# Both attention phases of neighbouring batches in common slots, in a decoder layer on one core

## What is computed

```python
x = _layernorm(x + _L0_attn_ref(x, ...))          # relu(x Wqkv); vk = v^T k; y = (vk q) / den; y Wp + b
x = _layernorm(x + _L0_xattn_ref(x, ctx_1024, ctx_1024, pos, pos, ...))
    # q = x Wq, k = ctx Wk, v = ctx Wv; q, k to float16 and rotated; softmax(q k^T / 4) v; Wo + b
x = _layernorm(x + _L0_ffn_ref(x, ...))           # x U1 V1 + b1, gelu, U2 V2 + b2
```

## Time and profile before

| | us |
|---|---|
| median of 3 runs | 634.99 (631.4 to 635.81) |
| profiled execution | 636.95 |
| its span, from the first to the last instruction | 635.0 |
| PE busy in the span | 555.6 |
| DVE busy | 464.2 |
| ACT busy | 312.4 |
| POOL busy | 286.8 |

### The profile page before, as it was taken

The page is one execution under the profiler, slowest core; times in us unless marked ns, Lnnn a source line. Parts: engine busy times, 40 slices in busy tenths (PEclk is TensorE's granted clock), DMA queues, the critical chain, the costliest instruction groups (busy, mean ns, idle before and its releaser), DMA issues.

```text
span 635.0 us, 12707 instructions
## 1 busy us (share of the span) xinstructions
PE 555.6 (87%) x4288; PEld 369.3 (58%) x4288; DVE 464.2 (73%) x974; ACT 312.4 (49%) x455; POOL 286.8 (45%) x300
## 2 busy tenths in 40 slices
PE   0867799899999999999999999999996958999993
PEld 0755557575757575766657575757573524455561
DVE  4377569898988888889889798989887672244434
ACT  4321173645545463646373736455454626656561
POOL 3471535454546454637364554545453401224334
PEclk9886599999999999999999999999999877999998
DMA  7526200201020202020201111010000000033322
GB/s 251 124 69 131 64 6 10 67 9 67 8 66 8 66 8 67 7 70 11 66 18 58 39 35 63 11 66 8 34 9 18 26 1 17 18 106 121 104 99 100
DMA packets 24029, 33.77 MB, mean 53 GB/s; under 512 B 4552, under 2 KB 10440, under 8 KB 24008
## 3 DMA queue, kind: packets, MB, share of 16 engines
q1 hardware_dynamic: 23192, 33.07, 17.2%
q10 hardware_dynamic: 816, 0.43, 0.3%
HBM read 22.73 MB, written 8.65 MB: 49 GB/s over the span
## 4 chain that ended last, share of the span: by engine, by line
PE 61%; issue 10%; DVE 9%; ACT 8%; POOL 4%; POOLq 0%; DVEq 0%; ACTq 0%
PE FR L1013 14%; PE BK L1013 12%; PE BK L1174 9%; PE SC L1157 5%; DVE nmax L857 5%; PE SC L1133 5%; ACT probs L634 3%; PE FR L1081 3%; PE FR L1089 3%; PE FR L1071 3%; PE FR L1215 3%; PE BK L1185 2%; POOL rs L536 2%; POOL c_fm L541 2%; ACT x_fm L623 2%
## 5 line engine op out<-in xcount | busy, mean ns | idle before, releaser
L857 DVE TENSOR_REDUCE nmax<-SC 128x4 f32<-128x1024 f32 x128 | 149.8, 1216 | 12.4 <-PE SC L1133 12.3
L634 ACT ACTIVATE probs<-SC 128x1024 f32<-128x1024 f32 x128 | 124.3, 1033 | 19.5 <-PE SC L1157 19.5
L1174 PE MATMUL BK<-probs,v_aug 128*32 128x256 f32 x1024 | 69.5, 389 | 0.0
L1133 PE MATMUL SC<-k_blk,q_grp 32*128 32x512 f16 x256 | 49.2, 402 | 12.6 <-DVE nmax L857 12.6
L442 POOL TENSOR_TENSOR att_fm_l<-att_raw,att_fm_h 128x512 fp32r<-128x512 f32 x16 | 20.6, 1286 | 74.1 <-ACT att_raw L615 74.1
L1157 PE MATMUL SC<-q_grp,k_blk 64*128 64x256 f16 x512 | 45.9, 279 | 9.0 <-ACT probs L634 8.4
L696 ACT ACTIVATE probs<-SC,b_ff 128x512 f32<-128x512 f32 x64 | 39.6, 688 | 24.4 <-PE SC L1338 23.7
L431 POOL TENSOR_TENSOR k_cos<-k,cos_t 128x512 f16<-128x512 f16 x16 | 18.5, 1154 | 69.4 <-ACT k L591 69.4
L1174 PEld LDWEIGHTS BK<-probs,v_aug 128*32 128x32 f32 x1024 | 26.9, 110 | 28.2 <-issue 10.9
L838 DVE TENSOR_SCALAR x_tm<-y,mv,rs 128x256 f32<-128x256 f32 x32 | 39.1, 1261 | 3.9 <-POOL rs L447 3.9
L1157 PEld LDWEIGHTS SC<-q_grp,k_blk 64*128 64x128 f16 x512 | 17.5, 95 | 34.6 <-ACT probs L634 26.5
(11 more groups left out here) (173 smaller groups left out, 1623.0 us busy)
## 6 DMA issues: line engine op xcount, KB each, us to landing
x_fm<-in_x_fm SPq DMA_DIRECT2D x16, 256.0 KB, 2.7
x_tm<-in_x_tm SPq DMA_DIRECT2D x16, 256.0 KB, 2.9
c_fm<-in_c_fm SPq DMA_DIRECT2D x16, 256.0 KB, 3.4
x_kept<-x2b SPq DMA_DIRECT2D x16, 256.0 KB, 2.1
x_tm<-x_kept SPq DMA_DIRECT2D x16, 256.0 KB, 2.7
out<-c_fm SPq DMA_DIRECT2D x16, 256.0 KB, 2.0
k_blk<-k_rope SPq DMA_DIRECT2D x128, 16.0 KB, 1.8
cos_t<-rope_tables SPq DMA_DIRECT2D x1, 896.0 KB
```

The source lines that it names most:

```text
L634: act.activation(probs[:, j % 4], SC[j % 2][:], ACT.Exp, scale=SCALE).then_inc(s_exp, 1)
L857: dve.tensor_reduce(nmax[:, t, HC * q:HC * q + HC], SC[c % 2][:], AX.X, ALU.max, negate=True).then_inc(s_max, 1)
L1133: mm = pe.matmul(SC[c % 2][:, 2 * s:2 * s + 2].rearrange("p h t -> p (h t)"), q_grp[par][rows, q, t * P:(t + 1) * P], k_blk[par][rows, q]. ...
L1174: mm = pe.matmul(BK[q // 2][HP * k:HP * (k + 1), (q % 2) * T:(q % 2 + 1) * T], v_aug[par][:, t, HC * q + k], probs[:, j % 4, k], start=(t ...
```

## The change

The steps go from -3 to 15, all written out, with no loop up to the feed-forward blocks. A step has 8 slots. In each slot PE makes a chunk of the **second scores of batch b** and, in every second slot, a pair of weighted sums, and then a chunk of the **first scores of batch b+1**; the rest follows behind them. So `SC[0]` (SA) serves the first scores alone and `SC[1]` (SB) the second ones alone: a chunk of first scores waits for the maximum of the chunk before, a chunk of second scores for the exponential of the chunk before.

```diff
+            def step(b):
+                n1, n, m, p, q, kn = b + 1, b + 2, b + 3, b - 1, b - 2, key_batch(b)
...
+                if on(b):
+                    scores2(b, 4)
+                    pv(b, 2)
+                    pv(b, 3)
+                if on(n1):
+                    scores1(n1, 5)
+                if on(m):
+                    lin(m, 0, q)
+                    lin(m, 1, q)
+
+                if on(b):
+                    scores2(b, 5)
+                if on(n1):
+                    scores1(n1, 6)
+                if on(kn):
+                    v2(kn, b)
+                if on(m):
+                    lin_t(m)
```

```diff
+            def rope_q_sum(n):
+
+                wait(dve, s_s2_mm, NQ * (n - 2))
+                dve.wait_ge(s_q_part, 2 * n + 2)
+                grp = q_grp[n % NB][:].rearrange("p (c e) t -> p e c t", e=2)
+                for s in range(2):
+                    src, dst = TR * s + PR, TR * s
+                    dve.tensor_tensor(grp[dst:dst + PR, 0], q_cos[dst:dst + PR], q_sin[dst:dst + PR], ALU.add)
+                    ins = dve.tensor_tensor(grp[dst:dst + PR, 1], q_cos[src:src + PR], q_sin[src:src + PR], ALU.add)
+                ins.then_inc(s_q_rope, 1)
...
+                if on(n1):
+                    row_max(n1, 5)
+                if on(p):
+                    add2(p)
+                if on(n):
+                    rope_q_sum(n)
+
+                if on(m):
+                    lin(m)
+                if on(n1):
+                    row_max(n1, 6)
...
             def residual2(n):
 
                 pool.wait_ge(s_x1, 2 * n + 2)
-                wait(pool, s_wo_ev, n - 1)
+                wait(pool, s_wo_ev, n - 2)
...
             def kv1(m, t):
 
                 if t == 0:
                     pe.wait_ge(s_xs, m + 1)
+                    wait(pe, s_proj_ev, m)
```

More of the change, by code:

```diff
@@ L520, in _ @@
[L520 to L527 removed]
+            for i in range(NB):
+                pool.memset(v_aug[i][:], 1.0).then_inc(s_v_ones, 1)
@@ new lines, in _ @@
+            for i in range(NB):
+                pool.memset(q_grp[i][:].bitcast(F32), 0.0).then_inc(s_q_zeros, 1)
+            for b in range(FIRST, 0):
+                step(b)
+                if b == -2:
+                    for k in (6, 7):
+                        pool.wait_ge(s_w_hi, k + 1)
+                        src, hi, lo = split[k]
+                        pool.tensor_tensor(lo, src, hi.bitcast(F32), ALU.subtract).then_inc(s_ff_lo, 1)
+            for b in range(0, B):
+                step(b)
@@ L692, in _ @@
+            for b in range(FIRST, 0):
+                step(b)
+                if b == -3:
+                    for k in range(N_MAIN, len(split)):
+                        weights_hi(k)
+            for b in range(0, B):
+                step(b)
+            exp_chunk(LAST, 7)
+            ev_pv(LAST, 1)
             act.sem_inc(s_gelu, 4)
@@ L708, in _ @@
             ev_att(LAST)
-            for f in range(2, NF):
+            gelu(0, 2)
+            gelu(0, 3)
+            ev_x2t(LAST - 1)
+            gelu(0, 4)
+            ev_p(LAST - 1)
+            for f in range(5, NF):
                 gelu(0, f)
@@ L980, in _ @@
+            for b in range(FIRST, B):
+                step(b)
             dve.sem_inc(s_qf_ev, 1)
             dve.sem_inc(s_y3, 2)
+            stats2(LAST - 1)
             att_norm(LAST)
-            add2(LAST, 1)
+            add2(LAST)
+            ev_p(LAST - 1)
             stats2(LAST)
@@ L1110, in x1_t, with lin_t, proj1 @@
-            def x1_t(n):
+            def lin_t(m):
+                if m == 0:
+                    pe.wait_ge(s_early_const, 32)
+                pe.wait_ge(s_lin_ev, 2 * m + 2)
+                turn(FR[0], lin_tm, s_lint_mm)
+            def proj1(m):
+                if m == 0:
+                    pe.wait_ge(s_w_lo, 5)
+                pe.wait_ge(s_lint_ev, m + 1)
+                for t in range(TT):
+                    mm = project(FR[1], lin_fm, w_p1, t)
+                mm.then_inc(s_proj_mm, 1)
@@ L1327, in _ @@
+            for b in range(FIRST, B):
+                step(b)
+            scores2(LAST, 7)
+            pv(LAST, 6)
+            pv(LAST, 7)
             o_t(LAST, 1)
@@ L1382, in _ @@
             h_ff(0, 5)
-            wo(LAST, 0)
-            wo(LAST, 1)
+            x2_t(LAST - 1)
+            wo(LAST)
+            p_ff(LAST - 1)
             u2_ff(0, 2)
```

996 lines of the change are left out of this document (454 added, 542 removed).

## The result

The changed kernel takes **701.8 us** (median; 700.48 to 703.26) beside 633.19 for the kernel before on the same chip: a ratio of 1.108, 95% interval 1.102 to 1.114. The forecast was 650.0 with a range of 622 to 671. The direction was right, the size was not: the time lies beyond even the rival in which POOL takes every turn (669).

The account below looks back on a forecast made before the run. PE was taken to bound the kernel before; afterwards a step of 28.2 + R, 31.3 us. 85 to step 0, 401.5 for thirteen steps and 67 to the last `o_t` made 553.5 against 538.66, so 650.0 us, range 622 to 671.

Parts of the forecast that it names:

- the rival in which POOL takes every turn: POOL gets its turn after each DVE addition: R = 4.45, step 32.7, 669 us; chance 0.17.
- Place and mechanism: PE's longest wait at `lin_t`, 2.4 us plus additions' loss; L848 and L849 take 0.5 to 1.4 us beside POOL.
- Unrolling at nothing: Writing the loop out as straight code was costed at nothing: step 13, already written out, took the loop's 30.0 us.
- Waits for exponentials gone: PE's waits for exponentials at second scores, about 0.6 and 0.2 us in a step before, would disappear.
- 48 rows at nothing: First scores of 48 rows in place of 32 cost nothing, since second scores use 64 rows and still pair.
- The step is 28.2 + R: Step chain: 20.0 for five slots, 4.2 + R on DVE, 4.05 behind `lin_t`; R is the time of `rope_q_sum`.
- R = 3.1: Four DVE additions of `rope_q_sum`: the middle of 1.7 (run through) and 4.45 (POOL after each); step 31.3 us.
- The PE clock: Low clock was charged 2.5 us in step -1 and 2 us in the end steps.
- Filling: Step 0 starts at 85, with batch 0's first scores at 58.9 and 1.9 us for `residual_bias(0)` behind `rope_k(0)`.
- The one in which PE is the bound: Additions end in time or unit costs are smaller; 27.2 us a step gives 597, halfway 615; chance 0.1.
- DVE's work after the change: DVE loses `norm1` (2.63 us) and a copy (0.7) to ACT, gains 0.4 in `rope_q_sum`: about 23.5 us a step.

Follow-up runs that it names:

- the clock held: Changed kernel with 32 idle weights-by-weights matmuls on PE ahead of `lin_t` in steps 0 to 12: 682.2 us.
- POOL's work moved: Changed kernel with one more wait: POOL starts `residual2(n)` only when `rope_q_sum(n)` is done: 652.45 us.
- another order on DVE and POOL: Changed kernel with DVE and POOL work reordered, filling queue positions moved, and `q1` first on PE with ACT's copies to match: 607.1 us.
- `lin` first: Changed kernel with `lin(m)` moved on DVE ahead of `add2(p)` and `rope_q_sum(n)`, behind `row_max` 5: 689.5 us.
- the filling edit alone: Changed kernel with POOL's `residual_bias(0)` and split of c(1) ahead of `rope_k(0)`, and the `x_fm(2)` load ahead of `place_k(0)`: 689.8 us.

## Why the prediction was wrong

By its own steps:

- **Place and mechanism: right.** PE's longest wait of a step is at `lin_t` on `lin_tm`; L849 and L848 take 0.74 to 1.42 us and end 0.3 us behind L476, L440 and L425. Unrolling at nothing: right within 2 us. Waits for exponentials gone: right. 48 rows at nothing: the first scores take 386 ns at the median, beside 384 before.
- **"The step is 28.2 + R": right, with a condition that I did not put.** At R 1.73 it gives 29.9, measured 30.1; at R 4.05 with the clock held 32.25, measured 32.4. It holds for a full clock. q_sin, too, took 1.38 us for 0.42 in each full step of the changed kernel, which the forecast left out; it does so with POOL's work moved as well, where the sum fits, so it cost the step nothing.
- **R = 3.1: too small.** I took the middle between two cases, the blocked q_sin and the unhindered additions beside `norm2`. Measured 4.02, near the upper bound of 4.45. Two of the three POOL instructions beside the additions have two inputs, as beside q_sin, and the case of one input said nothing on them. The nearer row should have decided. The third, L425, has one input and held an addition up all the same, by 0.3 us, more than the 0.1 read beside `norm2`; why is open. This is 0.9 us a step, 11 us in steps 1 to 12 (in step 0 the additions ran unhindered). The rule of the Trainium skill that the prediction names, "SBUF — State Buffer", section "Who interferes with whom", that the two exclude each other for the whole instruction, came closer with its 4.45 than my middle.
- **The PE clock: left out of the step.** This is the step of the prediction that failed most. I put a low clock on the filling and on the end steps, with the 0.72 of the earlier trace rows before me, but no clock on a gap that I myself had computed at 3.8 us (2.4 and what the additions lose). Measured: 0.50 behind each gap of 4.42 us, 1.8 us a step, 22 us over 12 steps. The two terms, 33, are nearly all of the 34.6 us that steps 0 to 12 took above the forecast; the last three steps gave 70.4 for 67.
- **Filling: 97.0 for 85.** This is the third step that failed. I charged `residual_bias(0)` behind `rope_k(0)` with 1.9 us. The wait at `add1` was 7.5, and it pushed batch 1 beside the weight splits, where the next 5 us were lost. Undone, step 0 starts at 84.3.
- **The rivals.** POOL at every turn was nearly what happened (669 with R 4.45), and lacked the clock as well. The one in which PE is the bound (597 to 615) describes what the change can do with another order on DVE and POOL: 607.
- **A slip without effect:** DVE's work after the change is 25.92 less 2.63 and 0.7 and 0.4 more, so 23.0 us and not 23.5; nothing in the sum rests on it.

In short, of the 68 us against the kernel before, POOL's company of four additions holds 49 (with the part of the clock that follows from it), the filling alone 12. The two overlap, since about 8 of the 49 lie ahead of step 1.

## What to carry to other kernels

When a wait moves to one place, ask how long PE stands still there at one stretch: here waits of up to 1.3 us cost their own length, and the one of 4.42 us cost 1.8 more, as the clock was at half for the 4 to 5 us behind it. When a wait is released, see what else it releases: here `add2` set POOL going in the moment in which DVE had its own critical instructions, and an extra wait on the engine with time to spare was worth 49 us. And price each queue position in the filling by what is behind it on its engine, not by its own length.

## What the runs showed that was not expected

- The same gap of 2.13 us on PE (2.12 in some steps) left the clock full behind six `lin_t` of the kernel with POOL's work moved, and brought it down behind five (transposes of 0.66, or of 0.87 to 1.12 us; steps of 30.1, or of 31.6), in no order that the rows explain. Gaps of 1.3 us did not bring it down in the runs here. Behind the twelve gaps of 3.66 or 3.67 us with `lin` first it fell each time, in two of them only behind the first scores (0.39 us at 244.93 and 412.15, then a granted clock of 0.53 in 246 to 248 and 0.50 in 414 to 416). Behind the 24 gaps of 4.32 to 4.43 us of the changed kernel and of the one with the filling edit alone it fell each time as well, in one of them late:

```profile
479.92 0.66 PE L1126 MATMUL FR<-ident,lin_tm 128*128 128x128 f32 x4 [4.43 <-DVE lin_tm L817]
...
480.86 1.93 PE L1210 MATMUL BK<-probs,v_aug 128*32 128x256 f32 x16
```

  So a full clock right behind a gap does not yet say that the gap was free. What decides at 2.13 stays open.
- A `tensor_scalar` of 32 columns took 1.25 us in place of 0.18 beside POOL's two-input subtraction of 1.26 us: its price was that of the other engine's instruction, seven times its own length.
- 32 idle matmuls a step made the kernel 19.6 us faster.
